# A graph layer pair on one core: first rows in smaller pieces, factors moved to GpSimd, conversions of the adjacency tiles one pair closer to their use

## The chip, the cores and the metric

The kernel runs on 1 core of a Trainium2 chip. The metric is the device time of one execution in microseconds (us). The profile shown is that of one execution of the kernel before.

## The reference

Inputs are x (4096 x 128, float32), adj (4096 x 4096, zeros and ones with the diagonal set), a scalar beta, and two 128 x 128 weights.

```python
h = relu(layernorm(x))
norm2 = norm(h, axis=1, keepdims=True)
cos = beta[0] * (h @ h.T) / (norm2 @ norm2.T + 1e-07)
P = softmax(cos + (1.0 - adj) * -1e9, axis=1)
x = x + P @ h
h = relu(layernorm(x))
deg = clip(sum(adj, axis=1, keepdims=True), 1.0)
x = x + h @ W_self + (adj @ h / deg) @ W_neigh
```

## The kernel before

Two stages follow each other. The first is an attention over the adjacency's edges, the second an aggregation `adj @ h` with two small products. TensorE works nearly all the time in both.

**The front.** x comes in four pieces of 8 tiles (a tile is 128 rows). VectorE computes mean and variance of each piece (`variances`, L640), GpSimd raises variance + eps to the power -1/2 (`inverse_std`, L376), VectorE multiplies by a constant factor and makes the bias (`scales`, L652), ScalarE makes the rows of h (L512), VectorE sums their squares (`norms`, L660), GpSimd raises these to -1/2 (`inverse_norm`, L382). A "unit" is a group of 4 tiles of h divided by their norms; there are 8, made by GpSimd (0, 7), ScalarE (3) and VectorE (the others). TensorE transposes each, ScalarE and VectorE split it into a high and a low 16-bit part (`unit_high` L503, `unit_low` L678). When all norms are known, their smallest one decides by a flag (`s_flag`, L437 to L442) which of two forms of the attention ScalarE and VectorE run. The general form is not run with these inputs. ScalarE's and VectorE's first attention instructions stand behind that flag. GpSimd also makes the low half of a table of h (`low_parts`, L369) after ScalarE has made the high half (`table_high`, L522).

**The attention** goes over 72 pairs k. The adjacency is symmetric in its use of the scores: a pair (s, p) joins 512 rows of step s with 256 rows of pair p. A pair whose rows lie in a later step is used in both directions ("far"), and has two 512 KB tiles of the adjacency, a near and a far one; a pair within its own step has only the near one. Step s starts at pair 0, 16, 30, 42, 52, 60, 66, 70. In step 0 the own pairs come first. In the later steps own pairs stand at the third and the fifth place of the step, pairs 18 and 20 in step 1.

For each k in turn:
- SP loads the near tile, and the far tile right behind it (L323 to L334). Near tiles have two slots, so the load of near tile k waits until near tile k-2 has been converted (L327).
- GpSimd converts near tile k+3 to fp8 behind its masking of pair k (`convert(k + LEAD)`, L479, with `LEAD = 3`), and every second far tile (`convert_far`). ScalarE converts the other far tiles (`convert`, L530): that of pair k+2 behind the exponentials of pair k (L588).
- TensorE computes the scores of pair k+2 (L941), multiplies the far words (L979 to L982), transposes words of pair k+1 (L952), multiplies the near words (L1002 to L1005).
- ScalarE computes the exponentials twice, in 16 and 32 bits (L561, L562). Those of pair k wait until GpSimd has masked pair k-2 (L552).
- VectorE subtracts them into a low part (`low_part`, L778), masks far words (`mask_far`, L788), adds finished far rows (L803). Its order for one k is low part of the first chunk of k+2, spill of k, `mask_far` of k+1, low part of the second chunk of k+2.
- GpSimd masks the near words (`mask_near`, L407). Behind it stand the table parts, the conversions, and at the fifth pair of a step (k = 20 in step 1) the five small instructions of `scales_of_x2` (L456).
- Score banks: the first score chunk of a pair waits for the low part of the last chunk two pairs before, the second for that of the first chunk of the pair before (`ring_free`, L909, where no unit stands between).

ScalarE's second layernorm (`second_h`) has its first half behind the exponentials of the seventh pair of a step (k = 22 in step 1), and its second half with `second_high` behind those of the eighth, k = 23, after the conversion that stands there.

Of the kernel before, what the change touches and what calls it, by code (L numbers as in the profile page):

```python
# [5 lines left out]
def gnn_program(nc, x_in, adj_in, beta_in, w_self_in, w_neigh_in, out):  # L6
# [7 lines left out]
    T = N // P  # L14
# [9 lines left out]
    RING = [("unit", 0), ("unit", 1), ("score", 0, 0), ("score", 0, 1), ("score", 1, 0), ("score", 1, 1), ("unit", 2)]  # L24
# [18 lines left out]
    XP = 4  # L43
    TX = T // XP
    LEAD = 3
# [6 lines left out]
    with ctx:  # L52
# [36 lines left out]
        var_e, rstd, scale_h, bias_h, norm2, norm2_g, rnorm, rnorm_s = [early(7, T) for _ in range(8)]  # L89
# [6 lines left out]
        def u_rows(a, b):  # L96
            half, lo = u_half[a * 2 // T], a * 2 // T * (T // 2)
            return half[:, (a - lo) * D:(b - lo) * D]

# [89 lines left out]
        def transpose_bank(g):  # L189

            return 5 + AT["unit", g] % 3
# [72 lines left out]
        s_rnorm_s = sem("rnorm_scaled")  # L264
# [47 lines left out]
        def _(sp):  # L312
            sp.dma_start(beta, beta_in.partition_broadcast(P)).then_inc(s_beta, 16)
            for i in range(XP):
                sp.dma_start(x_v3[:, TX * i:TX * (i + 1), 0:D], x_v[:, TX * i:TX * (i + 1), :]).then_inc(s_x[i], 16)

# [6 lines left out]
            tile = 0  # L323
            for k in range(NP):
                s = PAIR[k][0]
                if k >= 2:
                    sp.wait_ge(s_adjd, k - 1)  # L327
                sp.dma_start(stage[:, k % 2 * TILE:(k % 2 + 1) * TILE], adj_in[tile]).then_inc(s_near_in[k % 2], 16)
                tile += 1
                if PAIR[k][2]:  # L330
                    m = FAR_BEFORE[k]
                    if m >= 2:
                        sp.wait_ge(far_sem(m), m // 2)
                    sp.dma_start(stage[:, (2 + m % 2) * TILE:(3 + m % 2) * TILE], adj_in[tile]).then_inc(s_far_in[m % 2], 16)  # L334
                    tile += 1
# [20 lines left out]
        def _(pool):  # L356
# [19 lines left out]
            def inverse_std(i):  # L376

                part = slice(i * TX, (i + 1) * TX)
                pool.wait_ge(s_var, i + 1)
                pool.tensor_tensor(rstd[:, part], var_e[:, part], neg_half, ALU.pow).then_inc(s_rstd, 1)  # L380

            def inverse_norm(i):  # L382

                part = slice(i * TX, (i + 1) * TX)
                pool.wait_ge(s_norm2, i + 1)
                pool.tensor_tensor(rnorm[:, part], norm2_g[:, part], neg_half, ALU.pow).then_inc(s_rnorm, 1)

            def scaled_inverse_norm(i):

                pool.wait_ge(s_rnorm, i + 1)  # L390
                pool.tensor_scalar(rnorm_s[:, i * TX:(i + 1) * TX], rnorm[:, i * TX:(i + 1) * TX], HS, None, ALU.mult
                                   ).then_inc(s_rnorm_s, 1)
# [16 lines left out]
            def units(g):  # L409

                pool.wait_ge(s_rnorm, g * TPS // TX + 1)
                for t in range(g * TPS, (g + 1) * TPS):
                    pool.tensor_scalar(u_rows(t, t + 1), h_rows(t, t + 1), rnorm[:, t:t + 1], HS, ALU.mult, ALU.mult
                                       ).then_inc(s_unit_p, 1)

            def convert_far(k):
# [3 lines left out]
                if m == FAR_BEFORE[FIRST[2]]:  # L420
# [79 lines left out]
        def _(act):  # L500
# [7 lines left out]
            for i in range(XP):  # L508
                act.wait_ge(s_scales, i + 1)
                for t in range(i * TX, (i + 1) * TX):  # L510
# [3 lines left out]
                if i == XP - 2:  # L514
# [707 lines left out]
```

## Time and profile before

| | us |
|---|---|
| median of 3 runs | 504.44 |
| lowest, highest | 503.09, 505.62 |
| the profiled execution | 502.87 |
| its span, from first to last instruction | 500.9 |
| TensorE busy in the span | 471.2 |
| VectorE, ScalarE, GpSimd busy | 279.8, 298.1, 297.0 |

The 2.0 us between the span and the profiled execution's time lie around the first and the last instruction. An engine's busy time is an average over a front in which TensorE waits, an attention and an aggregation in which it does not; what matters for a change is where in the trace TensorE is idle.

### The profile page before, as it was taken

How to read it: one execution, taken by the hardware profiler on the slowest of the kernel's cores; microseconds unless marked ns; L12 is line 12 of the kernel's file. 1: busy time of each engine (PE TensorE's matmuls, PEld its weight loads, DVE VectorE, ACT ScalarE, POOL GpSimd, SP SyncE). 2: the span in 40 equal slices, each digit the busy share in tenths (PEclk: the TensorE clock that was granted, in tenths of full speed). 3: DMA queues.
4: the chain of work that ended last, by engine and by line, in shares of the span. 5: the costliest groups of instructions: out<-in, count | busy, mean ns of one | idle time of the engine just before them, and what ended most of it. 6: DMA issues, size and time to landing. Idle time of an engine off the chain costs nothing.

```text
span 500.9 us, 12746 instructions
## 1 busy us (share of the span) xinstructions
PE 471.2 (94%) x5392; PEld 397.7 (79%) x5392; DVE 279.8 (56%) x686; ACT 298.1 (60%) x427; POOL 297.0 (59%) x261
## 2 busy tenths in 40 slices
PE   0768999999999999999999999999799999999996
PEld 0636788888788888888888888877688888888895
DVE  6975666567566585656765856757632321322153
ACT  2979787866986759876798598688730201110121
POOL 3889887877897768986799688888750000000000
PEclk9989999999999999999999999999999999999999
DMA  8057865655776557754676476563010000000001
GB/s 248 12 183 282 273 204 175 224 178 183 252 249 221 181 161 249 245 217 157 225 244 236 167 227 223 205 196 107 3 34 1 22 22 22 1 22 22 22 1 43
DMA packets 31549, 74.39 MB, mean 149 GB/s; under 512 B 2560, under 2 KB 15104, under 8 KB 31488
## 3 DMA queue, kind: packets, MB, share of 16 engines
q1 hardware_dynamic: 31488, 73.54, 43.8%
q8 instruction: 42, 0.69, 0.6%
q14 instruction: 19, 0.16, 0.1%
HBM read 71.43 MB, written 2.10 MB: 147 GB/s over the span
## 4 chain that ended last, share of the span: by engine, by line
PE 87%; DVE 5%; POOL 3%; DMA 2%; ACT 2%; issue 1%; SPq 0%; POOLq 0%; DVEq 0%; ACTq 0%
PE ps L1078 23%; PE ps L941 17%; PE ps L952 9%; PE ps L1005 6%; PE ps L1002 6%; PE ps L1004 6%; PE ps L979 5%; PE ps L982 5%; PE ps L981 5%; PE ps L1063 2%; PE ps L1052 2%; DVE adj_t L665 1%; DVE adj_t L644 1%; DMA stage<-in_adj_dram 1%; DMA x_sb<-in_x_dram 1%
## 5 line engine op out<-in xcount | busy, mean ns | idle before, releaser
L407 POOL TENSOR_TENSOR near<-word,adj_t 128x1024 f32<-128x1024 f32 x72 | 145.2, 2016 | 57.4 <-DVE word L778 56.4
L561 ACT ACTIVATE word<-ps,small 128x512 f16<-128x512 f32 x144 | 135.6, 942 | 70.8 <-PE ps L941 67.0
L778 DVE TENSOR_TENSOR word<-ps,word 128x512 f16<-128x512 f32 x144 | 106.3, 739 | 105.4 <-ACT ps L562 105.3
L1078 PE MATMUL ps<-table,adj_t 128*128 128x257 f16 x1024 | 116.8, 274 | 0.0
L941 PE MATMUL ps<-unit_t 128*128 128x512 f16 x432 | 106.7, 381 | 4.7 <-DVE word L778 4.7
L1078 PEld LDWEIGHTS ps<-table,adj_t 128*128 128x128 fp8e4 x1024 | 99.3, 98 | 13.0
L562 ACT ACTIVATE ps<-ps,small 128x512 f32<-128x512 f32 x144 | 107.2, 744 | 0.0
L1002 PE MATMUL ps<-table,near 128*128 128x129 f16 x576 | 102.6, 219 | 4.0 <-POOL near L407 2.6
L1005 PE MATMUL ps<-table,near 128*128 128x129 f16 x576 | 102.8, 222 | 0.0
L1004 PE MATMUL ps<-table,near 128*128 128x128 f16 x576 | 102.6, 219 | 0.0
L979 PE MATMUL ps<-table,far 128*128 128x129 f16 x448 | 79.9, 219 | 0.3
L982 PE MATMUL ps<-table,far 128*128 128x129 f16 x448 | 80.0, 222 | 0.0
L981 PE MATMUL ps<-table,far 128*128 128x128 f16 x448 | 79.8, 219 | 0.0
L788 DVE TENSOR_TENSOR far<-ps,adj_t 128x1024 f32<-128x1024 f32 x56 | 68.4, 1222 | 14.0 <-PE ps L952 14.0
L398 POOL TENSOR_SCALAR adj_t<-stage 128x1024 uint8<-128x1024 f32 x72 | 75.4, 1047 | 0.6
L616 ACT ACTIVATE stage<-ps 128x1024 f16<-128x1024 f16 x15 | 14.6, 1021 | 101.8 <-PE ps L1052 101.8
L941 PEld LDWEIGHTS ps<-unit_t 128*128 128x128 f16 x432 | 39.4, 98 | 41.6 <-DVE word L778 7.9
L1002 PEld LDWEIGHTS ps<-table,near 128*128 128x128 f16 x576 | 57.0, 99 | 6.4 <-POOL near L407 2.7
L952 PE MATMUL ps<-ident,word 128*128 128x128 f32 x448 | 58.3, 273 | 0.0
L1004 PEld LDWEIGHTS ps<-table,near 128*128 128x128 f16 x576 | 55.9, 97 | 2.0
L1005 PEld LDWEIGHTS ps<-table,near 128*128 128x128 f16 x576 | 56.3, 98 | 0.0
L979 PEld LDWEIGHTS ps<-table,far 128*128 128x128 f16 x448 | 44.4, 99 | 10.4 <-DVE far L788 5.7
(94 smaller groups left out, 490.6 us busy)
## 6 DMA issues: line engine op xcount, KB each, us to landing
stage<-in_adj_dram SPq DMA_DIRECT2D x128, 512.0 KB, 4.4
x_sb<-in_x_dram SPq DMA_DIRECT2D x4, 512.0 KB, 6.2
x_again<-in_x_dram SPq DMA_DIRECT2D x8, 256.0 KB, 5.6
out_dram<-x_sb SPq DMA_DIRECT2D x7, 256.0 KB, 2.3
out_dram<-x_sb SPq DMA_DIRECT2D x1, 192.0 KB, 2.0
stage<-in_L_gnn_W_neigh_dram SPq DMA_DIRECT2D x1, 64.0 KB, 2.6
stage<-in_L_gnn_W_self_dram SPq DMA_DIRECT2D x1, 64.0 KB, 2.5
out_dram<-x_sb SPq DMA_DIRECT2D x1, 64.0 KB, 1.7
```

The source lines that it names most:

```text
L407: pool.tensor_tensor(ring(near, k), ring(word, k), adj_t[:, near_adj(k)], ALU.mult).then_inc(s_near, 1)
L561: act.activation(half(word16, k, c, 0, HIGH, TPS), score(k, c), ACT.Exp, bias=exp_bias, scale=exp_scale)
L562: act.activation(score(k, c), score(k, c), ACT.Exp, bias=exp_bias, scale=exp_scale).then_inc(s_exp, 1)
L778: dve.tensor_tensor(half(word16, k, c, 0, LOW, TPS), score(k, c), half(word16, k, c, 0, HIGH, TPS), ALU.subtract).then_inc(s_elo, 1)
L941: ins = pe.matmul(score(k, c), j, rows, start=i == 0, stop=i == 2)
L979: pe.matmul(far_acc(c), high, tab(rows, D, TW), start=c == 0 and t == 0, stop=False, skip_group_check=True)
L981: pe.matmul(far_acc(c, 0, D), high, tab(rows, 0, D), start=False, stop=False, skip_group_check=True)
L982: last = pe.matmul(far_acc(c), low, tab(rows, D, TW), start=False, stop=t == TPS - 1, skip_group_check=True)
L1002: pe.matmul(acc(s, t), high, tab(rows, D, TW), start=first and c == 0 and t % 2 == 0, stop=False, skip_group_check=True)
L1004: pe.matmul(acc(s, t, 0, D), high, tab(rows, 0, D), start=False, stop=False, skip_group_check=True)
L1005: last = pe.matmul(acc(s, t), low, tab(rows, D, TW), start=False, stop=end and c == 1, skip_group_check=True)
L1078: return pe.matmul(ps[:, agg_bank(g) + t, 0:TW], adj_t[:, at:at + P], tab(b), start=(b == 0), stop=(b == T - 1))
```

## The change

x is loaded in five pieces, two of 4 tiles and three of 8. The constant factors of the inverse deviation and the inverse norm move into an instruction of GpSimd ahead of each power, so that VectorE's and GpSimd's separate scaling instructions go. Units 0, 5 and 6 are made by ScalarE (5 and 6 inside the attention), 1 to 4 by VectorE (3 and 4 behind the flag), 7 by GpSimd at k = 6. The first table part is made ahead of the flag, and the later ones one pair earlier or later than before on GpSimd. The first two far tiles are loaded with the first two near ones. The first three transposes use other banks. `LEAD` goes from 3 to 2.

```diff
-    RING = [("unit", 0), ("unit", 1), ("score", 0, 0), ("score", 0, 1), ("score", 1, 0), ("score", 1, 1), ("unit", 2)]
+    RING = [("score", 0, 0), ("score", 0, 1), ("score", 1, 0), ("score", 1, 1)]
...
-    XP = 4
-    TX = T // XP
-    LEAD = 3
+    PIECE = [slice(0, 4), slice(4, 8), *(slice(t, t + 8) for t in range(8, T, 8))]
+    XP = len(PIECE)
+    GROUPS = [p.stop // TPS for p in PIECE]
+    LEAD = 2
...
+            load_near(0)
+            load_near(1)
+            load_far(FAR[0])
+            load_far(FAR[1])
+            for k in range(2, NP):
+                sp.wait_ge(s_adjd, k - 1)
+                load_near(k)
+                m = FAR_BEFORE[k]
+                if PAIR[k][2] and m >= 2:
+                    sp.wait_ge(far_sem(m), m // 2)
+                    load_far(k)
...
             def inverse_std(i):
-                pool.tensor_tensor(rstd[:, part], var_e[:, part], neg_half, ALU.pow).then_inc(s_rstd, 1)
+                pool.tensor_scalar(var_e[:, part], mv_v[:, part, 1], HS ** -2, EPS * HS ** -2, ALU.mult, ALU.add
+                                   ).then_inc(s_scaled_e, 1)
+                pool.wait_ge(s_scaled_e, i + 1)
+                pool.tensor_tensor(scale_h[:, part], var_e[:, part], neg_half[:, 0:part.stop - part.start], ALU.pow
+                                   ).then_inc(s_rstd, 1)
...
             inverse_std(2)
             inverse_norm(0)
-            units(0)
+            inverse_norm(1)
             inverse_std(3)
-            inverse_norm(1)
-            scaled_inverse_norm(1)
             convert(0)
+            inverse_std(4)
             inverse_norm(2)
+            convert(1)
...
+            low_parts(0)
             inverse_norm(3)
-            units(7)
-            convert(1)
-            convert(2)
-            convert_far(2)
+            inverse_norm(4)
...
                 mask_near(k)
-                if s == 0 and k % 2 == 0:
-                    low_parts(k // 2)
+                if k == 1:
+                    convert_far(2)
+                if s == 0 and k % 2 == 1 and (k + 1) // 2 < NS:
+                    low_parts((k + 1) // 2)
+                if k == 6:
+                    units(7)
                 if k + LEAD < NP:
                     convert(k + LEAD)
-                    if PAIR[k + LEAD][2] and FAR_BEFORE[k + LEAD] % 2 == 0:
+                    if k >= 1 and PAIR[k + LEAD][2] and FAR_BEFORE[k + LEAD] % 2 == 0:
                         convert_far(k + LEAD)
...
+            first_h(0, 0, 4)
+            first_h(1, 4, 8)
+            first_h(2, 8, 12)
+            units(0)
+            first_h(2, 12, 16)
+            unit_high(0)
+            first_h(3, 16, 24)
+            first_h(4, 24, T)
+            act.wait_ge(s_h, TPS)
+            table_high(0)
             act.wait_ge(s_flag, 1)
...
-                    if k == 1:
-                        unit_high(2)
+                    if k <= 1:
+                        unit_high(k + 1)
...
+                    if k in (3, 5):
+                        units((k + 7) // 2)
...
             norms(0)
             scales(2)
+            norms(1)
             variances(3)
-            norms(1)
             scales(3)
+            variances(4)
             norms(2)
-            units(1)
             unit_low(0)
+            scales(4)
             norms(3)
+            norms(4)
...
-            unit_low(1)
-            units(2)
+            units(1)
             dve.wait_ge(s_flag, 1)
             any_small = dve.value_load(small_norm[0:1, :], min_val=0, max_val=1)
-            units(4)
-            units(5)
-            units(6)
+            units(2)
...
                     low_part(k, 0)
+                    units(3 + k)
                     low_part(k, 1)
-                unit_low(2)
+                    unit_low(1 + k)
...
-            sum_of_h(0, TX)
+            sum_of_h(0, 8)
             unit_transpose(0)
-            sum_of_h(TX, T - TX)
+            sum_of_h(8, 16)
+            scores(0)
+            for i in range(3):
+                score_product(1, 0, i)
+            sum_of_h(16, T)
             unit_transpose(1)
-            scores(0)
-            sum_of_h(T - TX, T)
-            scores(1)
-            unit_transpose(2)
+            for i in range(3):
+                score_product(1, 1, i)
...
                     scores(k + 2)
+                    if k == 0:
+                        unit_transpose(2)
```

## Rows read from the trace of the kernel before

**Rows 1.** The page: TensorE's busy time and share.
```profile
PE 471.2 (94%) x5392; PEld 397.7 (79%) x5392; DVE 279.8 (56%) x686; ACT 298.1 (60%) x427; POOL 297.0 (59%) x261
```

**Rows 2.** Windows: stretch, its length, busy us per engine, clock, DMA share, GB/s.
```profile
50.00:60.00 10.00, 10.00 (x125) 8.40 (x123) 6.14 (x10) 7.96 (x11) 9.03 (x7) 1.00 0.81 285
```

**Rows 3.** Timeline of the front: start us, us, engine, line, operation, count.
```profile
5.59 1.64 DVE L644 BATCH_NORM_STATS2 adj_t<-x_sb 128x6 f32<-128x128 f32 x8 [0.59 <-DMA x_sb<-in_x_dram]
7.27 0.64 DVE L647 BATCH_NORM_AGGREGATE adj_t<-adj_t 128x2 f32<-128x6 f32 x8
...
10.88 9.35 ACT L512 ACTIVATE adj_t<-x_sb,adj_t 128x128 f32<-128x128 f32 x24 [8.86 <-DVE adj_t L657]
...
20.99 3.19 ACT L512 ACTIVATE adj_t<-x_sb,adj_t 128x128 f32<-128x128 f32 x8 [0.28 <-DVE adj_t L657]
...
27.08 0.15 DVE L710 TENSOR_SCALAR small<-small 128x1 f32<-128x1 f32 x1
...
28.80 0.92 ACT L561 ACTIVATE word<-ps,small 128x512 f16<-128x512 f32 x1 [1.52 <-POOL small L441]
```

**Rows 4.** GpSimd by line and form: count, busy us, mean ns, idle before.
```profile
L407 POOL TENSOR_TENSOR near<-word,adj_t 128x1024 f32<-128x1024 f32 x72 | 145.2, 2016 | 57.4 <-DVE word L778 56.4 <-PE ps L1005 0.9
L398 POOL TENSOR_SCALAR adj_t<-stage 128x1024 uint8<-128x1024 f32 x72 | 75.4, 1047 | 0.6
L424 POOL TENSOR_SCALAR adj_t<-stage 128x1024 uint8<-128x1024 f32 x28 | 29.3, 1046 | 0.0
L373 POOL TENSOR_TENSOR table<-adj_t,table 128x512 f16<-128x512 f32 x8 | 9.1, 1133 | 0.0
...
L465 POOL TENSOR_TENSOR small<-small 128x4 f32<-128x4 f32 x8 | 8.1, 1014 | 0.7
L386 POOL TENSOR_TENSOR adj_t<-adj_t,small 128x8 f32<-128x8 f32 x4 | 6.6, 1660 | 0.7 <-DVE adj_t L669 0.6
...
L391 POOL TENSOR_SCALAR adj_t<-adj_t 128x8 f32<-128x8 f32 x1 | 0.3, 288 | 0.1
```

**Rows 5.** Timeline: one VectorE instruction beside a conversion on GpSimd.
```profile
22.62 1.05 POOL L398 TENSOR_SCALAR adj_t<-stage 128x1024 uint8<-128x1024 f32 x1
...
22.69 1.01 DVE L669 TENSOR_SCALAR adj_t<-adj_t 128x8 f32<-128x8 f32 x1
```

**Rows 6.** The far tiles' loads, L334: time from issue to landing.
```profile
DMA to landing us min/median/max: 3.7/4.7/6.9
```

**Rows 7.** Timeline of step 1 on GpSimd, ScalarE and VectorE, pairs 21 to 24.
```profile
133.17 1.05 POOL L398 TENSOR_SCALAR adj_t<-stage 128x1024 uint8<-128x1024 f32 x1
...
136.40 2.01 POOL L407 TENSOR_TENSOR near<-word,adj_t 128x1024 f32<-128x1024 f32 x1
...
138.44 0.93 ACT L561 ACTIVATE word<-ps,small 128x512 f16<-128x512 f32 x1 [0.47 <-POOL near L407]
...
141.33 1.06 ACT L538 ACTIVATE adj_t<-stage 128x1024 uint8<-128x1024 f32 x1
...
143.72 0.91 ACT L561 ACTIVATE word<-ps,small 128x512 f16<-128x512 f32 x1
...
145.26 0.74 DVE L778 TENSOR_TENSOR word<-ps,word 128x512 f16<-128x512 f32 x1 [2.43 <-ACT ps L562]
...
146.23 1.20 DVE L788 TENSOR_TENSOR far<-ps,adj_t 128x1024 f32<-128x1024 f32 x1
```

**Rows 8.** The chain that ended last, in steps 0 and 1: start, us, what.
```profile
50.33 1.41 PE ps L941 x6
...
147.06 1.29 PE ps L941 x6
```

**Rows 9.** Timeline at the like places of steps 2 and 6.
```profile
206.25 1.06 ACT L538 ACTIVATE adj_t<-stage 128x1024 uint8<-128x1024 f32 x1
...
333.65 1.05 POOL L398 TENSOR_SCALAR adj_t<-stage 128x1024 uint8<-128x1024 f32 x1
...
337.56 1.10 ACT L538 ACTIVATE adj_t<-stage 128x1024 uint8<-128x1024 f32 x1
```

More of the change, by code:

```diff
@@ L88, in gnn_program @@
         mv = early(7, T * 2)
-        var_e, rstd, scale_h, bias_h, norm2, norm2_g, rnorm, rnorm_s = [early(7, T) for _ in range(8)]
+        var_e, scale_h, bias_h, norm2, norm2_g, rnorm = [early(7, T) for _ in range(6)]
         ones_w = early(6, P)
@@ L98, in u_rows, with piece_of @@
             return half[:, (a - lo) * D:(b - lo) * D]
+        mv_v = mv.rearrange("p (t c) -> p t c", c=2)
+        def piece_of(g):
+            return min(i for i in range(XP) if GROUPS[i] > g)
         def by_tile(ap):
@@ L189, in transpose_bank @@
         def transpose_bank(g):
[L191 removed]
+            return (3, 4, 2)[g] if g < 3 else 5 + AT["unit", g] % 3
         def tab(t, lo=0, hi=TW):
@@ L321, in load_x_again, with load_near, load_far @@
                 sp.dma_start(by_tile(x_again[:, :]), x_v[:, s * TPS:(s + 1) * TPS, :]).then_inc(s_xr, 16)
[L323 to L335, printed above, removed]
+            def load_near(k):
+                sp.dma_start(stage[:, k % 2 * TILE:(k % 2 + 1) * TILE], adj_in[k + FAR_BEFORE[k]]).then_inc(s_near_in[k % 2], 16)
+            def load_far(k):
+                m = FAR_BEFORE[k]
+                sp.dma_start(stage[:, (2 + m % 2) * TILE:(3 + m % 2) * TILE], adj_in[k + m + 1]).then_inc(s_far_in[m % 2], 16)
+            load_near(0)
[5 more added lines that the diff above has]
+                load_near(k)
+                m = FAR_BEFORE[k]
+                if PAIR[k][2] and m >= 2:
+                    sp.wait_ge(far_sem(m), m // 2)
+                    load_far(k)
                 for again in range(NS):
@@ L642, in variances @@
                 dve.wait_ge(s_x[i], 16)
-                for t in range(i * TX, (i + 1) * TX):
+                for t in range(PIECE[i].start, PIECE[i].stop):
                     last = dve.bn_stats(stats[:, t * 6:(t + 1) * 6], x_row(t))
                 then(last)
-                for t in range(i * TX, (i + 1) * TX):
+                for t in range(PIECE[i].start, PIECE[i].stop):
                     last = dve.bn_aggr(mv[:, t * 2:(t + 1) * 2], stats[:, t * 6:(t + 1) * 6])
-                then(last)
-                dve.tensor_scalar(var_e[:, i * TX:(i + 1) * TX], mv_v[:, i * TX:(i + 1) * TX, 1], EPS, None,
-                                  ALU.add).then_inc(s_var, 1)
+                last.then_inc(s_var, 1)
             def scales(i):
-                part = slice(i * TX, (i + 1) * TX)
+                part = PIECE[i]
+                dve.wait_ge(s_var, i + 1)
                 dve.wait_ge(s_rstd, i + 1)
-                then(dve.tensor_scalar(scale_h[:, part], rstd[:, part], HS, None, ALU.mult))
                 dve.scalar_tensor_tensor(bias_h[:, part], mv_v[:, part, 0], -1.0, scale_h[:, part],
@@ L660, in norms @@
             def norms(i):
-                part = slice(i * TX, (i + 1) * TX)
-                for t in range(i * TX, (i + 1) * TX):
+                for t in range(PIECE[i].start, PIECE[i].stop):
                     dve.wait_ge(s_h, t + 1)
@@ L667, in norms @@
                         scale=1.0, scalar=0.0, op0=ALU.mult, op1=ALU.add, accum_out=norm2[:, t:t + 1])
-                then(last)
-                dve.tensor_scalar(norm2_g[:, part], norm2[:, part], 1e-20, None, ALU.max).then_inc(s_norm2, 1)
+                last.then_inc(s_norm2, 1)
             def units(g):
-                dve.wait_ge(s_rnorm, g * TPS // TX + 1)
+                dve.wait_ge(s_rnorm, piece_of(g) + 1)
                 for t in range(g * TPS, (g + 1) * TPS):
-                    dve.tensor_scalar(u_rows(t, t + 1), h_rows(t, t + 1), rnorm[:, t:t + 1], HS,
-                                      ALU.mult, ALU.mult).then_inc(s_unit, 1)
+                    dve.tensor_scalar(u_rows(t, t + 1), h_rows(t, t + 1), rnorm[:, t:t + 1], None, ALU.mult).then_inc(s_unit, 1)
             def unit_low(g):
```

59 lines of the change are left out of this document (30 added, 29 removed).

## The prediction

> **What bounds the kernel now.** I read the busy times, then the windows, then the timeline of the front, then one later step engine by engine. TensorE is busy 471.2 of 500.9 us [rows 1], and from about 50 us on a window of the attention is full, 10.00 of 10.00, with ScalarE at 7.96 and GpSimd at 9.03 [rows 2]. The change leaves TensorE's work as it is. So there are only two ways to the time: the point at which TensorE's unbroken work begins moves, or a stall opens in it. As marker of the first I take the end of the scores of pair 5, 50.33 + 1.41 = 51.74 [rows 8].
>
> The reader is to see in the later step [rows 7] how close the helpers run. GpSimd masks pair 21 from 136.40 to 138.41, ScalarE had waited 0.47 us for it and begins its exponentials of pair 23 at 138.44, converts the far tile of pair 25 at 141.33 without a wait, and starts pair 24 at 143.72. A far tile takes 4.7 us (3.7 to 6.9) from issue to landing [rows 6]. Conversions are made three pairs ahead, so this tile was asked for well before.
>
> **Part 1: the front.** The time of a piece follows its parts. VectorE's statistics of 8 tiles take 7.27 + 0.64 - 5.59 = 2.3 us [rows 3], of 4 tiles 1.25. A power is 1.66 us for 8 columns and 1.01 for 4; with the factor instruction now ahead of it (0.29) and the hops between, 2.15 and 1.4 [rows 4]. The first piece is half as large, so VectorE can start between 5.0 and 5.59; I take 5.0.
> - Statistics of piece 0 to 6.3, power to 7.7, first row of h at 8.0, against 10.88 [rows 3].
> - Piece 1: power to 9.0. Piece 2: statistics to 10.2, power to 12.35. GpSimd then makes the powers of norms 0 and 1, to 15.0. These are one more than before at this place.
> - Piece 3: VectorE does its statistics behind the norms of piece 1, to 15.7; power to 17.9. VectorE now stands in `scales(3)` and waits for it, since the statistics of piece 4 come behind. They end at 20.4, their power at 22.55, and ScalarE makes the last eight rows from 22.9, 3.19 long [rows 3], to 26.1. Before they ended at 20.99 + 3.19 = 24.18.
> - The last squares, the minimum and its sign take 0.8 more: 26.9, against 27.08 + 0.15 = 27.23 [rows 3]. So the early start of 2.9 us is used up before the flag. I call this point L.
>
> One thing can make L later. An 8-column instruction of VectorE took 1.01 us and ended with a 1.05 us conversion of GpSimd beside it [rows 5]; the one of L710 took 0.15 [rows 3]. The moved `convert(1)` now runs beside VectorE's norms, so L lies between 26.9 and 26.9 + 1.0. I take 27.2.
>
> The Trainium skill (SBUF — State Buffer, Who interferes with whom) speaks against this placing: the second port pair is an exclusive lock that GpSimd shares with two-input instructions of VectorE, and the later one blocks fully. The row agrees in size. By the rule L would be 27.9 and the total 0.7 higher; without it 0.3 lower.
>
> From L on GpSimd is the longer way. It has, one behind the other [rows 3, 4]: the flag 0.7 (estimated from 27.23 to ScalarE's start at 28.80, of which the flag is the first half), a table part 1.13, two powers of 2.07, masking of pair 0 2.02, a conversion 1.05, masking of pair 1 2.02, a far conversion 1.05, a table part 1.13, conversion of tile 3 1.05. Sum 14.2, thus 41.4. Only then are near and far tile 5 asked for. Issue 0.4 and landing 4.7 [rows 6] give 46.5, ScalarE's conversion 1.0 gives 47.5. From the start of the exponentials to the second low part VectorE needs (145.26 - 143.72) + (146.23 - 145.26) + 1.20 + 0.65 = 4.4 [rows 7], and the second half of the scores 0.65. The marker falls at 52.5, against 51.74: **0.8 later**, with L's bounds 0.5 to 1.5, and down to -0.5 if the tile lands in 3.7.
>
> Units 5 and 6 on ScalarE are four activations of 0.4 each (3.19 / 8) [rows 3], 1.6 a time. The first four stand ahead of the wait for tile 5, which hides them; uncovered they cost 1.6. The second four, at pair 5, delay ScalarE by less than it idles per pair (10.00 - 7.96 in ten us, [rows 2]) and VectorE's `mask_far` of the pair before is later than they are: 0, uncovered 1.6. Unit 7 on GpSimd is under 2 us at pair 6, where masking has several us before TensorE needs it: 0, uncovered 2. VectorE loses two to three small instructions a piece, which is in the sum above; units 3 and 4 behind the flag run while it waits for exponentials. The two early far tiles remove nothing at the marker, since tile 5 is later.
>
> **Part 2: LEAD 3 to 2.** SP asks for near tile k, and the far one behind it, when tile k-2 is converted. That conversion stood behind the masking of pair k-5 and now stands behind that of pair k-4. ScalarE's conversion of far tile k stands behind its exponentials of k-2, which themselves need only the masking of k-4. So exponentials (141.33 - 138.44 = 2.89 us) run against conversion, issue and landing (1.05 + 0.4 + 4.7 = 6.15). Where ScalarE starts right when the mask ends, it waits 3.2 us. In the regular part it starts some 3.5 us behind the mask, which leaves a wait of a few tenths in its idle time: 0. Behind the two own pairs of a step, where TensorE needs little time, it starts at once (the 0.47 of rows 7).
>
> Step 1 in full [rows 7]. At pair 20 GpSimd converts till 134.22, then makes the five small instructions of the second layernorm, and masks pair 21 at 136.40. With the new lead a far conversion (1.05) belongs here too: pair 22's instead of none. Mask 21 runs 137.45 to 139.46, conversion of 23 to 140.5, far tile 25 is issued at 140.9 and lands at 145.6. ScalarE converts it to 146.55; the second layernorm's rows behind it take 143.72 - 141.33 - 0.96 = 1.43; pair 24 starts at 148.0 instead of 143.72, 4.3 later. VectorE's low part moves from 145.26 to 149.55, its far masking to 150.5, with end at 151.7. TensorE was ready for that product at 147.06 + 1.29 = 148.35 [rows 8]. Loss: **3.35 us**. Bounds: without the extra far conversion 2.3, with landing in 3.7 another 1.0 less, thus 1.3; with 6.9 it is 5.5.
>
> The same place is there in steps 2, 3 and 4 (first 206.25, [rows 9]), the pattern of pairs being the same: 4 x 3.35 = 13.4. In step 6 the tile of pair 68 is behind a conversion that ends at 333.65 + 1.05 = 334.7, and lands at 339.8, 2.2 us after ScalarE asks for it at 337.56 [rows 9]. The helpers bound there already: **2.2** (0 to 3.3).
>
> **Sum.** 502.87 + 0.8 + 13.4 + 2.2 = 519.3 for the profiled execution. The median of the runs is 1.57 above that execution, so I move halfway, to **520**.
>
> **The rivals.**
> - The tiles come sooner. Landing in 3.7 and no push of mask 21 by the far conversion give 1.3 a step, 1.2 in step 6 and 0.3 in front: 502.87 + 5.2 + 1.5 = 509.6, with the half step to the median 510. For: 3.7 occurs; against: that the far load goes out right behind the near one here. Chance 0.18.
> - The waits are there and hidden. TensorE has scores two pairs ahead, so ScalarE might catch up: only the front's 0.8 is left, 504 to 505. For: no wait of TensorE in these windows before; against: VectorE's 1.20 us far masking ends at 147.4, only 0.9 ahead of TensorE's need. Chance 0.12.
> - Faster: the early rows carry through. h starts 2.9 us sooner; if the fifth piece follows without VectorE's wait in `scales(3)` and tile 5 is there in time, the whole front moves, 504.4 - 2.9 = 501.5. It decides at the flag: it must come at 25 us or earlier, and the steps must not stall. For: 10.88 becomes 8.0; against: the last row's 26.1. Chance 0.08.
> - The tiles come later still, near 6.9, as near and far share the DMA engines: 5.5 a step, 527. Chance 0.07.
> - My forecast: 0.55, own range 515 to 523.
>
> Faster and slower are counted from 0.5%, 2.5 us, about what a measurement of this kernel can tell from no change. Faster 0.08; same 0.12; slower 0.55 + 0.18 + 0.07 = 0.80. The range is 506 to 523: it leaves out the hidden and the faster case at the low end. They hold 0.20.
>
> **What would show it.** Each step: first h row at 8.0; last at 26.1; ScalarE's L538 waits for the DMA 3 us or more at the conversions of pairs 25, 39, 51 and 61, and about 2 at 68; TensorE then waits for VectorE's `far` (L788) some 3 us, four times; the other windows stay full. Wrong it is if ScalarE's conversions show no wait for the DMA, or if they wait and TensorE's gaps don't grow, or if the flag comes before 25 us.

## The result, and the profile after

The changed kernel takes 534.07 us (532.20 to 535.95, 6 runs) against 504.31 (502.81 to 505.62, 6 runs): a ratio of 1.0595, interval 1.0574 to 1.0617. The forecast was 520 with a range of 506 to 523. The sign was right, the size was not: 30 us were lost, not 16. The profiled execution took 532.20 us, its span 530.4 against 500.9. Of all 79 recorded executions of the kernel before, all but four lie in one of two groups, 502.6 to 503.4 us and 504.1 to 504.8, and its profiled one is of the lower.

The page after, its busy times and the head of its chain of waits, to be read beside [rows 1]:

```profile
PE 483.0 (91%) x5392; PEld 403.1 (76%) x5392; DVE 279.4 (53%) x671; ACT 299.8 (57%) x435; POOL 298.5 (56%) x268
...
PE 63%; POOL 9%; DVE 9%; DMA 8%; ACT 5%; issue 4%; SPq 0%; ACTq 0%; POOLq 0%; DVEq 0%
```

TensorE has the same 5392 products and is counted busy for 483.0 us instead of 471.2. So of the 29.5 us of span, 17.7 are idle time, and in 11.8 the same products take longer. The ends of products are modelled in a profile, so the 11.8 are no clean measure of any one cause; what the lower clock costs is worked out below from starts. The transfers of the adjacency now make 8% of the chain.

Where the time went is read best from one event that both kernels have 72 times, the start of ScalarE's exponentials (L561 before, L591 after). This is the delay against before in us, worked out from the timelines; the last row is the end of the span. The other columns are experiments of the next section.

```
                        forecast  after   e1     e2     e3     e4
after the front (k=6..20)   0.8    5.98   3.48   2.65   3.02   3.87
gained in step 1 (k=27)     3.35   5.60   0.00   5.64   0.40   4.72
gained in step 2 (k=43)     3.35   3.25   0.00   3.27   1.80   3.34
gained in step 3 (k=53)     3.35   3.86   0.00   3.57   0.35   3.78
gained in step 4 (k=62)     3.35   5.71   0.00   5.48   0.48   3.36
gained in step 6 (k=69)     2.2    3.36   0.28   2.24   0.66   3.24
the rest, to the end        0      1.7   -0.2    0.4    0.2    0.4
```

**The stalls are where they were forecast.** ScalarE's conversions of far tiles by line, and the five that were named (start, length, and in brackets the wait and what ended it):

```profile
L568 ACT ACTIVATE adj_t<-stage 128x1024 uint8<-128x1024 f32 x28 | 29.7, 1061 | 31.1 <-DMA stage<-in_adj_dram 31.0
```

```profile
152.31 1.06 ACT L568 ACTIVATE adj_t<-stage 128x1024 uint8<-128x1024 f32 x1 [3.89 <-DMA stage<-in_adj_dram]
...
221.78 1.06 ACT L568 ACTIVATE adj_t<-stage 128x1024 uint8<-128x1024 f32 x1 [2.83 <-DMA stage<-in_adj_dram]
...
280.68 1.06 ACT L568 ACTIVATE adj_t<-stage 128x1024 uint8<-128x1024 f32 x1 [2.90 <-DMA stage<-in_adj_dram]
...
330.68 1.06 ACT L568 ACTIVATE adj_t<-stage 128x1024 uint8<-128x1024 f32 x1 [4.22 <-DMA stage<-in_adj_dram]
...
365.36 1.06 ACT L568 ACTIVATE adj_t<-stage 128x1024 uint8<-128x1024 f32 x1 [3.02 <-DMA stage<-in_adj_dram]
```

They are the tiles of pairs 25, 39, 51, 61 and 68, 16.9 of the 31.0 us of waiting. The other eleven waits, 14.1 us together, are not in the forecast's sum. They seem to have fallen mostly into time in which ScalarE is otherwise idle, for steps 2 and 3 lost about what was forecast. The chain of waits of the changed kernel in step 1 (start, us, what) goes just the way of the forecast, from GpSimd's masking over its conversion and the load to ScalarE and to VectorE's far masking:

```profile
143.43 2.00 POOL near L424
...
145.50 1.06 POOL adj_t L415
146.58 0.33 SPq L333
146.95 5.33 DMA stage<-in_adj_dram
152.31 1.06 ACT adj_t L568
153.37 0.78 ACT unit_t L599 x2
...
157.26 1.14 DVE far L814
```

The far load went out at 146.95: the forecast had 140.9, and with the front's 5.98 that is 146.9. It took 5.33 us against an assumed 4.7.

**What the forecast has no term for** is in the windows of the same place (stretch, its length, busy us of PE, PEld, DVE, ACT, POOL, then the clock that TensorE was granted, the DMA share and GB/s):

```profile
150.00:152.00 2.00, 2.00 (x32) 1.99 (x30) 0.00 (x0) 0.00 (x0) 2.00 (x2) 1.00 0.93 315
152.00:154.00 2.00, 1.83 (x24) 1.22 (x21) 0.00 (x0) 1.69 (x3) 1.55 (x2) 1.00 0.98 375
154.00:156.00 2.00, 0.00 (x0) 0.00 (x0) 0.00 (x0) 1.97 (x4) 0.00 (x0) 1.00 0.82 207
156.00:158.00 2.00, 0.82 (x3) 0.21 (x3) 1.77 (x3) 2.00 (x4) 0.00 (x0) 0.97 0.87 344
158.00:160.00 2.00, 1.55 (x15) 1.55 (x16) 1.78 (x3) 2.00 (x4) 0.88 (x1) 0.50 0.06 23
```

TensorE does nothing from 154 to 156 and little to 158. Work resumes, and now the granted clock is 0.50, the lower of its two levels (1.2 instead of 2.4 GHz). What that does to the work is seen best on equal work. TensorE's timeline shows 24 far products and then the transposes, first here and then in e4, an experiment of the next section in which the clock stays at 1.00 in this place:

```profile
158.45 0.29 PE L1009 MATMUL ps<-table,far 128*128 128x129 f16 x1 [0.61 <-DVE far L814]
...
161.01 1.19 PE L982 MATMUL ps<-ident,word 128*128 128x128 f32 x8
```

```profile
156.78 0.23 PE L1016 MATMUL ps<-table,far 128*128 128x129 f16 x1 [0.61 <-DVE far L814]
...
158.17 1.04 PE L989 MATMUL ps<-ident,word 128*128 128x128 f32 x8
```

From the first far product to the transposes it is 2.56 us here and 1.39 there. In step 4 and behind the last pair the clock falls too. The last two rows show the latter place: TensorE is idle from 388 to 390, and then the clock is 0.50:

```profile
334.00:336.00 2.00, 0.61 (x2) 0.28 (x3) 1.39 (x3) 2.00 (x4) 0.00 (x0) 0.85 0.75 305
336.00:338.00 2.00, 2.00 (x14) 1.18 (x13) 1.94 (x3) 2.00 (x4) 0.51 (x1) 0.50 0.00 0
...
388.00:390.00 2.00, 0.00 (x0) 0.00 (x0) 1.86 (x8) 1.88 (x5) 2.00 (x2) 1.00 0.00 0
390.00:392.00 2.00, 1.94 (x19) 1.94 (x20) 1.06 (x8) 0.41 (x1) 1.36 (x4) 0.50 0.35 107
```

**The front**, against [rows 3], in the timeline of the changed kernel (the rows follow each other by engine: ScalarE, VectorE, GpSimd):

```profile
8.35 1.65 ACT L532 ACTIVATE adj_t<-x_sb,adj_t 128x128 f32<-128x128 f32 x4 [6.32 <-DVE adj_t L686]
...
23.91 3.19 ACT L532 ACTIVATE adj_t<-x_sb,adj_t 128x128 f32<-128x128 f32 x8 [1.46 <-DVE adj_t L686]
```

```profile
18.19 1.04 DVE L686 SCALAR_TENSOR_TENSOR adj_t<-adj_t 128x8 f32<-128x8 f32 x1 [2.11 <-POOL adj_t L398]
...
28.41 0.15 DVE L739 TENSOR_SCALAR small<-small 128x1 f32<-128x1 f32 x1
...
35.82 2.76 DVE L702 TENSOR_SCALAR adj_t<-adj_t 128x128 f32<-128x128 f32 x4
```

```profile
18.17 1.05 POOL L415 TENSOR_SCALAR adj_t<-stage 128x1024 uint8<-128x1024 f32 x1
...
35.12 2.00 POOL L424 TENSOR_TENSOR near<-word,adj_t 128x1024 f32<-128x1024 f32 x1
...
37.20 1.11 POOL L415 TENSOR_SCALAR adj_t<-stage 128x1024 uint8<-128x1024 f32 x1
```

The first row of h comes at 8.35 (forecast 8.0), the last at 27.1 (26.1), the point L at 28.56 (27.2, before 27.23). And the four instructions of unit 4, which take 0.86 us elsewhere, take 2.76 beside a mask and a conversion of GpSimd. Unit 3 took 0.86.

### The profile page after: what moved, and what is told of

The parts are those of the page before. It is cut to its first block, busy times and chain, and to the rows that moved or that the text cites. A ratio compares the mean times of both kernels' runs of the same rounds, so it can differ in the third digit from the quotient of the medians.

```text
span 530.4 us, 12752 instructions
## 1 busy us (share of the span) xinstructions
PE 483.0 (91%) x5392; PEld 403.1 (76%) x5392; DVE 279.4 (53%) x671; ACT 299.8 (57%) x435; POOL 298.5 (56%) x268
## 4 chain that ended last, share of the span: by engine, by line
PE 63%; POOL 9%; DVE 9%; DMA 8%; ACT 5%; issue 4%; SPq 0%; ACTq 0%; POOLq 0%; DVEq 0%
PE ps L1112 21%; PE ps L971 9%; DMA stage<-in_adj_dram 7%; PE ps L982 6%; POOL near L424 5%; PE ps L1035 4%; PE ps L1009 4%; PE ps L1032 4%; PE ps L1012 4%; PE ps L1034 4%; PE ps L1011 3%; ACT word L591 3%; DVE far L814 2%; PE ps L1097 2%; POOL adj_t L415 2%
## 5 line engine op out<-in xcount | busy, mean ns | idle before, releaser
L591 ACT ACTIVATE word<-ps,small 128x512 f16<-128x512 f32 x144 | 134.6, 935 | 65.5 <-PE ps L971 60.9
L971 PE MATMUL ps<-unit_t 128*128 128x512 f16 x432 | 111.3, 390 | 22.5 <-DVE word L804 17.7
L1032 PE MATMUL ps<-table,near 128*128 128x129 f16 x576 | 103.8, 221 | 4.1 <-POOL near L424 2.8
L1035 PE MATMUL ps<-table,near 128*128 128x129 f16 x576 | 104.0, 224 | 0.0
L1034 PE MATMUL ps<-table,near 128*128 128x128 f16 x576 | 103.8, 221 | 0.0
L1009 PE MATMUL ps<-table,far 128*128 128x129 f16 x448 | 83.0, 224 | 3.7 <-DVE far L814 3.3
L1012 PE MATMUL ps<-table,far 128*128 128x129 f16 x448 | 82.9, 227 | 0.0
L1011 PE MATMUL ps<-table,far 128*128 128x128 f16 x448 | 82.8, 224 | 0.0
```

What stands on the lines that cost most here:

```text
L591: act.activation(half(word16, k, c, 0, HIGH, TPS), score(k, c), ACT.Exp, bias=exp_bias, scale=exp_scale)
L971: ins = pe.matmul(score(k, c), j, rows, start=i == 0, stop=i == 2)
L1009: pe.matmul(far_acc(c), high, tab(rows, D, TW), start=c == 0 and t == 0, stop=False, skip_group_check=True)
L1011: pe.matmul(far_acc(c, 0, D), high, tab(rows, 0, D), start=False, stop=False, skip_group_check=True)
L1012: last = pe.matmul(far_acc(c), low, tab(rows, D, TW), start=False, stop=t == TPS - 1, skip_group_check=True)
L1032: pe.matmul(acc(s, t), high, tab(rows, D, TW), start=first and c == 0 and t % 2 == 0, stop=False, skip_group_check=True)
```

## The experiments

My theory after the result had two parts. (a) `LEAD = 2` is nearly all of it: the far tile's load goes out too late, since it stands on SP behind a near load that waits for a conversion; a stall costs more than its idle time, because TensorE's clock falls behind it. (b) The front loses the rest, by the later L and by units on VectorE beside GpSimd's masks. The main rival of (a) was contention: two more tiles in flight, or the other edits of the attention, and not the lead.

**e1: the whole change but with three pairs of lead**, with the third conversion ahead of the loop as before.

```diff
-    LEAD = 2
+    LEAD = 3
...
             inverse_norm(4)
+            convert(2)
```

> The changed kernel with LEAD back at 3 (the conversion of tile 2 stands ahead of the loop again), all else as changed. Theory (the far tile that ScalarE waits for is asked for one pair too late): ScalarE's waits for the DMA at pairs 25, 39, 51, 61 and 68 go, and with them the 11.58 - 5.98 = 5.6, 3.25, 3.9, 5.7 and 3.35 us that these steps lose in the changed kernel, and most of the 1.8 at the end; what stays is the front's loss of up to 6 us. That gives 508 to 511 us. Rival (the steps' loss comes from the moved units, table parts or factors): the time stays above 525.

Measured: 508.36 (506.48 to 510.11), ratio 1.0092, interval 1.0060 to 1.0125. The steps lose nothing but 0.28 in step 6 (column e1); what is left is the front's 3.5. The lead is 534.07 - 508.36 = 25.7 us of the 29.8.

**e2: the reverse, only the lead changed in the kernel before.**

```diff
-    LEAD = 3
+    LEAD = 2
...
             convert(1)
-            convert(2)
-            convert_far(2)
```

> The kernel before with LEAD = 2 alone (conversion of tiles 2 and far 2 inside the loop). Theory: the steps lose what they lose in the changed kernel, 20 to 24 us, and the front little: 524 to 530 us. Rival (the loss needs the new order of the other work): under 510.

Measured: 530.39 (526.08 to 533.46), ratio 1.0542, interval 1.0491 to 1.0593. The median lies 0.4 above my bound. ScalarE's conversions in it, by line:

```profile
L536 ACT ACTIVATE adj_t<-stage 128x1024 uint8<-128x1024 f32 x28 | 29.7, 1062 | 35.9 <-DMA stage<-in_adj_dram 35.9
```

35.9 us of waiting, where the changed kernel has 31.0. The contention rival falls: none of the other edits is in this kernel, and its steps lose nearly the same amounts. The granted clock fell in steps 1 and 4 here too, and those two cost 5.6 and 5.5 against 3.3 and 3.6 for steps 2 and 3.

**e3: two pairs of lead, but SP asks for the far tile ahead of the near one.** The conversions stay as late as in the changed kernel, only the far load no longer stands behind the near load's wait.

```diff
-                sp.wait_ge(s_adjd, k - 1)
-                load_near(k)
                 m = FAR_BEFORE[k]
                 if PAIR[k][2] and m >= 2:
                     sp.wait_ge(far_sem(m), m // 2)
                     load_far(k)
+                sp.wait_ge(s_adjd, k - 1)
+                load_near(k)
```

> The changed kernel with LEAD = 2, but SP issues the far tile's load ahead of the near tile's wait, so that it hangs on its own slot alone and no longer on GpSimd's conversion of near tile k-2. Theory: it is the position of the load in SP's queue, not GpSimd's later conversion by itself, that makes ScalarE wait. The waits of ScalarE for the DMA at L568 go to about 0, and the time to 508 to 513 (front 4 to 6, and about 1 a step for the mask that a far conversion pushes). Rival (GpSimd's later conversions and masks hold ScalarE and TensorE): above 525.

Measured: 512.04 (509.64 to 513.61), ratio 1.0168, interval 1.0134 to 1.0202. 22 of the 25.7 us come back by a change of order in one queue. The far load of pair 25 goes out at 139.60 in SP's timeline, and the near one, now behind it, waits for its own slot till 143.58 without holding this far load up; below it ScalarE's conversions by line, with 5.0 us of waiting instead of 31.0:

```profile
139.60 0.50 SPq L338 DMA_DIRECT2D stage<-in_adj_dram  x1
143.58 0.33 SPq L333 DMA_DIRECT2D stage<-in_adj_dram  x1
```

```profile
L568 ACT ACTIVATE adj_t<-stage 128x1024 uint8<-128x1024 f32 x28 | 29.9, 1066 | 5.1 <-DMA stage<-in_adj_dram 5.0
```

What is left against e1, some 3.7 us, is the price of conversions one pair nearer to their use. The rest was the far load's place in the queue.

**e4: does the clock's fall have a price of its own?** In steps 1 and 4 the same stall is left, but TensorE repeats score products (12 more, ahead of the scores of pairs 25 and 61, into a bank that these overwrite), so that it is idle for less of it.

```diff
+                    if k in (23, 59):
+                        ring_free("score", k + 2, 0)
+                        for _ in range(4):
+                            for i in range(3):
+                                score_again(k + 2, 0, i)
                     scores(k + 2)
```

> The changed kernel in which TensorE repeats the first chunk's score products four times (12 matmuls, 2.6 us at full clock) ahead of the scores of pairs 25 and 61, the places of steps 1 and 4 where it otherwise stands idle 3 us and its granted clock falls to 0.50. The repeats write the same values and are not in the reference's work. Theory (steps 1 and 4 lose 5.6 and 5.7 us against 3.25 and 3.9 in steps 2 and 3 because of the clock): the clock stays at 1.0, each of the two steps loses 3.3 to 3.8, and the kernel is about 4 us faster than the changed one, 530 us. Rival (those two steps lose more because their tile lands later): no gain, 534 to 535.

Measured: 527.56 (525.38 to 529.50), ratio 1.0479, interval 1.0442 to 1.0515: 6.5 us faster than the changed kernel with 24 products more. The windows of this kernel in step 1:

```profile
154.00:156.00 2.00, 1.00 (x5) 0.21 (x3) 1.45 (x3) 2.00 (x4) 0.00 (x0) 1.00 0.90 332
156.00:158.00 2.00, 1.39 (x23) 1.23 (x23) 1.93 (x3) 2.00 (x3) 0.56 (x1) 1.00 0.14 55
```

The granted clock stays 1.00. The price of the clock can be read from how a step's delay goes on behind its stall: first the delay of the first exponentials behind it (pair 24, 38 or 60), then that of the pairs after (27, 43, 62), each gained within its step, in us, from the timelines.

```
clock fell to 0.50:   after, step 1  5.00 -> 5.60    after, step 4  5.48 -> 5.71
                      e2, step 1     4.98 -> 5.64    e2, step 4     4.75 -> 5.48
clock stayed at 1.00: after, step 2  3.96 -> 3.25    e2, step 2     3.96 -> 3.27
                      e4, step 1     5.43 -> 4.72    e4, step 4     4.03 -> 3.36
```

Where the clock stays, 0.7 us of the delay is made up again. (Step 3 isn't in the list: the clock stays there too, and 0.45 is made up in each of the three runs, from a first delay that reads 0.2 too small, since pair 50 starts that much sooner than in the kernel before in the kernels without a stall as well.) Where it falls, 0.2 to 0.7 is added. So a fall costs 0.9 to 1.4 us beside the idle time, in the changed kernel 1.3 in step 1 and 0.9 in step 4: 2.2, where I had expected 4. The starts of equal work say the same of step 1: from the first far product to the next near one 3.59 us at the lower clock, 2.27 in e4. The rest of the 6.5 us isn't the filler's: in this execution the tile of pair 61 came 1.4 us sooner and that of pair 25 0.4 later, and the clock stayed up in the front and behind the last pair too, where this kernel's code is the changed kernel's (1.6 and 1.4 us; 0.5 more in the front is an earlier tile, with which TensorE's idle time there is shorter by as much). So the same code may or may not be followed by the low clock. That the filler is what kept it up in steps 1 and 4 is likely, since it fell in both steps in the changed kernel and in e2, but one profile of each kernel doesn't show it.

**e5 to e7: the front, with three pairs of lead.** e5 moves VectorE's units 3 and 4 behind both low parts, to let GpSimd's masks start sooner:

```diff
                     low_part(k, 0)
-                    units(3 + k)
                     low_part(k, 1)
                     unit_low(1 + k)
+                    units(3 + k)
```

e6 is e5 with `convert_far(2)` at k = 0 instead of 1. e7 is e6 with `variances(4)` ahead of `scales(3)`, so that VectorE doesn't stand in the wait of 2.11 us shown above.

> The changed kernel with LEAD = 3, and VectorE's units 3 and 4 moved behind both low parts and the unit's low half. In the run with LEAD = 3 alone units 4 took 3.50 us for four instructions beside GpSimd's masking of pair 0 and a conversion (0.86 to 0.88 where nothing of that kind ran), which held the low part, mask 1, far conversion 2 and with them the load of tile 5. Theory: those 2.6 us are on the front's path; mask 1 comes 2 us sooner, ScalarE's wait of 2.30 us for tile 5 mostly goes, the front's loss falls from 3.5 to about 1.5 us: 506.0 to 506.8. Rival (tile 5 is late because of SP's order behind far tile 4, whatever the units do): no gain, 508.

> As the run before, with the conversion of far tile 2 behind mask 0 instead of mask 1, in GpSimd's idle time. SP's load of far tile 4 waits for it, and near and far tile 5 stand behind that load. Theory: far tile 5 is asked for another 2 us sooner and ScalarE waits for nothing: 505 to 506. Rival (the front's loss is the later flag, 28.4 against 27.2, alone): no difference to the run before.

> As the run before, with VectorE's statistics of the last piece ahead of scales(3) instead of behind it, so that it does not wait 2.1 us for the power of piece 3 with the statistics undone. Theory: the last row of h is there about 2 us sooner (25.0 instead of 27.1), the flag too, and the front gains 1.5 to 2: 503 to 504.5, as fast as the kernel before or slightly faster. Rival (GpSimd's chain of powers behind the flag sets the front, and these powers wait for norms that come no sooner): no gain.

Measured: e5 508.80 (507.47 to 509.23), e6 509.25 (507.50 to 509.46), e7 506.43 (505.26 to 507.43). e5 and e6 brought nothing against e1's 508.36: my theory that the units only had to stand behind the low parts fell. The timeline of VectorE in e7, then GpSimd's, shows what stands there in its place:

```profile
37.52 4.75 DVE L703 TENSOR_SCALAR adj_t<-adj_t 128x128 f32<-128x128 f32 x4
```

```profile
37.10 1.04 POOL L415 TENSOR_SCALAR adj_t<-stage 128x1024 uint8<-128x1024 f32 x1
38.10 1.99 POOL L424 TENSOR_TENSOR near<-word,adj_t 128x1024 f32<-128x1024 f32 x1
40.06 1.12 POOL L388 TENSOR_TENSOR table<-adj_t,table 128x512 f16<-128x512 f32 x1
41.15 1.04 POOL L415 TENSOR_SCALAR adj_t<-stage 128x1024 uint8<-128x1024 f32 x1
```

Four instructions of 0.21 us take 4.75 us, and they end as GpSimd's fourth one does, which looks like one of theirs for each of its. Moved behind the low parts they only met more of GpSimd's work. e7 gained 2.8 us on e6, of which the earlier L is 2.2 (26.45 instead of 28.61), and missed the 503 to 504.5 that I gave it. That the units are why is the theory that e9 tests.

**e8: the early first far tiles alone, in the kernel before.**

```diff
+            load_near(0)
+            load_near(1)
+            load_far(FAR[0])
+            load_far(FAR[1])
+            for k in range(2, NP):
```

> The kernel before with one part of the change alone: the first two far tiles are loaded with the first two near ones, ahead of any wait. In the kernel before ScalarE waited 1.46 us for far tile 3 in the front, on the chain that ended last. Theory: that wait goes and TensorE's unbroken work begins 1 to 1.4 us sooner: 502.9 to 503.4. Rival (the next tiles' loads or conversion 2 then bind at once): within 0.3 us of 504.3.

Measured: 503.25 (501.86 to 504.72), ratio 0.9986, interval 0.9972 to 1.0000. From pair 5 on the exponentials start 0.7 us sooner than before. A wait of 1.46 us for the second far tile is gone. In the median that is at the edge of what can be told from nothing. In e8's profile the clock falls behind the last pair and 1.6 us is lost there, as in the changed kernel's profile, though none of its steps stalls. The profiles of e10, e11 and e12 have that fall too; those of the kernel before, e1 to e7 and e9 don't.

**e9 and e10: the units away from the masks.** Unit 3 directly behind unit 2, unit 4 by ScalarE at k = 1; e9 starts from e7 with e5's move taken back, e10 from e1. ("The run before the last", in what was expected of e9, is e7.)

```diff
             units(2)
+            units(3)
...
-                    units(3 + k)
...
-                    if k in (3, 5):
+                    if k in (1, 3, 5):
                         units((k + 7) // 2)
```

> The changed kernel with three pairs of lead, the fifth piece's variances before scales(3) and the far conversion at pair 0 (as the run before the last), but units 3 and 4 no longer on VectorE beside GpSimd's masks: unit 3 is made right behind unit 2, unit 4 by ScalarE at pair 1. Theory (units on VectorE beside long GpSimd instructions cost about one such instruction each, 4.7 us for four on the way to the second low part): most of those 4.7 us goes, exponentials of pair 7 on start within 1 us of the kernel before, 502.5 to 504.0. Rival (the units only filled time in which VectorE waited for something else, and four activations of 0.4 us on ScalarE now delay it by as much): 505.5 to 507.0, as in the run that it starts from (506.4).

> The changed kernel with three pairs of lead (508.4) and only the same move of units 3 and 4. It parts the front's loss of 3.5 to 3.7 us in two: by the theory the units' share is about 2.5 us and the later flag's about 1.2, so 505.3 to 506.3 here. Rival (the later flag and the powers behind it are the whole loss): 507.5 to 509.

Measured: e9 504.20 (503.57 to 506.05), ratio 1.0012, interval 0.9995 to 1.0029; e10 506.03 (505.23 to 508.28), ratio 1.0050, interval 1.0032 to 1.0068. Against e7 and e1 that is 2.2 and 2.3 us. e9's rival falls, and its interval stays clear of e7's (1.0033 to 1.0069). e10's median lies where the theory has it, but its interval overlaps e1's, and its profile doesn't confirm the gain: the exponentials there lag by 4.35 us behind the front, more than e1's 3.48, with the clock at 0.50 from 46 to 48, where e1's stayed at 1.00. So e9 carries this result. e9 lies 0.2 above my bound: ScalarE is now busy in all of the 2 us windows from 38 to 50, with the four activations (1.26 us) among its work.

**e11: unit 4 on VectorE again, but beside GpSimd's power.** As e9, without ScalarE's unit at k = 1, and with these lines:

```diff
                     low_part(k, 0)
+                    if k == 0:
+                        units(4)
                     low_part(k, 1)
```

> As the run before (units 3 and 4 not beside masks, 504.2), but unit 4 is made by VectorE again, between the two low parts of pair 0, where GpSimd raises 128x8 to a power instead of masking. Theory (it is the long two-input and one-input instructions of GpSimd that hold VectorE up, its powers don't): the four take 0.9 to 1.1 us here, the low part behind them is hidden by GpSimd's powers, and ScalarE is rid of four activations (1.26 us) ahead of the exponentials of pair 2: 502.8 to 503.8. Rival (any GpSimd instruction holds the units up): the four take 1.9 us or more, and the run is at 504 or above.

VectorE's row of the unit, and GpSimd's two beside it:

```profile
30.47 0.86 DVE L703 TENSOR_SCALAR adj_t<-adj_t 128x128 f32<-128x128 f32 x4
```

```profile
30.42 0.36 POOL L405 TENSOR_SCALAR adj_t<-adj_t 128x8 f32<-128x8 f32 x1
30.86 1.79 POOL L408 TENSOR_TENSOR adj_t<-adj_t,small 128x8 f32<-128x8 f32 x1
```

0.86 us for the four: a power of GpSimd doesn't hold them up, the masks and conversions did. In its profile the exponentials of pair 2 start 1.16 us sooner than in e9 and those of pair 7 1.1 sooner, as expected. The median, 504.45 (503.35 to 505.00), ratio 1.0005, interval 0.9991 to 1.0019, doesn't confirm a gain over e9 (1.0012): the intervals overlap. The effect on the unit is shown, its worth is not.

**e12: e11 with ScalarE's order at k = 1 changed**: the table part and the conversion run where it waited 1.84 us for the transposes of unit 2.

```diff
-                    if k <= 1:
-                        unit_high(k + 1)
+                    if k == 0:
+                        unit_high(1)
...
                         convert(k + 2)
+                    if k == 1:
+                        unit_high(2)
```

> As e11, and ScalarE's high part of unit 2 behind its table part and conversion of pair 1 instead of ahead of them, since it waited 1.74 us there for TensorE's transposes. If ScalarE is what sets the front after the units are gone (100% busy from 38 to 51 us), the exponentials of pair 2 start 1 to 1.6 us sooner: 501.5 to 502.6, faster than both kernels. Rival: the later unit 2 holds up the scores of pair 4 and gives it back, 503 or above.

```profile
34.77 1.09 ACT L569 ACTIVATE adj_t<-stage 128x1024 uint8<-128x1024 f32 x1
36.38 0.60 ACT L526 ACTIVATE unit_t<-ps 128x512 f16<-128x512 f32 x1 [0.53 <-PE ps L964]
36.87 0.92 ACT L592 ACTIVATE word<-ps,small 128x512 f16<-128x512 f32 x1
```

ScalarE's timeline shows the wait down to 0.53 and the exponentials of pair 2 at 36.87, against 38.62 in the kernel before. From pair 6 on it leads the kernel before by 1.07 us. The median is 503.44 (501.95 to 504.85), ratio 0.9984, interval 0.9969 to 1.0000. That is 30.6 us better than the changed kernel. Against the kernel before it is about the same lead as e8's, at the edge of what can be told.

## Why the prediction was right in sign and wrong in size

I go through the prediction's steps in the profiled execution, whose span grew by 29.5 us; 16.4 were forecast and 13.1 are missing. The missing part falls into four pieces: 3.8 us of lower clock in the front and two steps, 4.0 in the steps' tiles, 3.6 in the front beside the clock, and 1.7 behind the last pair, nearly all of it a fall of the clock that the change need not have caused.

- **The late far load: right.** Place, cause and order of events were as forecast, in all five places, and the term of 3.35 measured 3.25 and 3.86 in steps 2 and 3. e1 and e2 show that the lead is the cause, e3 that it works through the far load's place behind the near load's wait. The hidden rival fell: ScalarE did not catch up.
- **The sentence that failed: "The change leaves TensorE's work as it is. So there are only two ways to the time"**, a later start or a stall. There was a third, the same products at half the clock behind a stall, and the sum has no term for it. It is 1.3 in step 1, 0.9 in step 4 and 1.6 in the front: 3.8 of the missing 13.1. Another 1.4 is the fall behind the last pair. That one needs no stall: e8, e10, e11 and e12 have it in their profiles with no step stalled. e8 is the kernel before but for its first loads, so that the profiled execution of the kernel before had none is likely chance. [Rows 2] show a window at 1.00: there was no long stall behind which the clock could fall, and the sum took every duration from there.
- **Tiles that came later than 4.7 us: 4.0 more over the steps.** The far tile of pair 25 took 5.33 and the first exponentials behind it came 5.0 late, not 4.3; that of pair 61 was waited for 4.22 us, that of pair 68 3.02 instead of 2.2 (step 6: 3.4 instead of 2.2). Without the clock each term lies within its bounds in the forecast (up to 5.5), save step 6's 3.36, just above 3.3. The 4.7 was the median of all landings in [rows 6]. From the start of their issue the five tiles took 5.3, 4.3, 4.4, 5.9 and 5.8 us, so it was fair for pairs 39 and 51 and short for the three others. The issuing instructions of those three lasted 0.97, 1.35 and 1.31 us in SP's timeline, against 0.43 and 0.44. Why is open; in e4 the tile of pair 61 landed in 4.5.
- **Part 1, the front: 0.8 forecast, 6.0 measured**, 4.4 without the clock, the term that was furthest off. GpSimd's chain of work, given till 41.4, ended at 44.45. Of this, 1.4 are L (28.56 instead of 27.2), and 1.0 is a wait of GpSimd for the low part that stood behind unit 4. I had given one conversion of GpSimd beside VectorE's squares a price (up to 1.0, of which I took 0.3). Two conversions struck: `scales(3)` took 1.04 instead of 0.19, and one square 1.16 instead of 0.28.
- **"Units 3 and 4 behind the flag run while it waits", priced at nothing: wrong.** Unit 4 took 2.76 beside the masks. Taking both units away from there gave back 2.2 us in e9, which had the conversions three pairs ahead. [Rows 5] had shown the effect on one small instruction. I applied it to the squares and not to the units, which are four instructions, each of which can be caught.
- **The range.** Its top of 523 is not worked out in the prediction, and its own rival of late tiles, 527 at a chance of 0.07, lay above it. 534 is nearest to that rival. A clock term for five stalls, about 1 us each, would have taken the rival to 532.
- From the profiled execution to the median the runs lie 1.9 us higher (534.07 against 532.20). The profiled execution was the fastest of the six and had the highest mean granted clock, 0.983 against 0.971 to 0.978. So in the others the lower clock probably cost more than the trace shows; no trace of them was kept.

## What to carry to other kernels

A load whose buffer is free must not stand in a queue behind one that waits: order the two by when their buffers come free, before you shorten a lead. Where a change opens a stall in TensorE's work, add to the idle time a price for running at 1.2 GHz behind it, here 0.9 to 1.4 us for each fall in a step. And ask of each VectorE instruction between buffers of SBUF that moves which GpSimd instruction will run beside it: the four instructions of one unit took 0.86 us beside a power and 4.75 beside a mask, a table part and two conversions.

And before two profiles are subtracted, look for events that one execution happened to have and the other not, as the fall of the clock behind the last pair: 1.4 of the 29.5 us here.

## What the runs showed of the hardware

- The clock after a stall isn't a matter of the idle time alone. In the changed kernel TensorE is idle for 2.93 us in the windows from 282 to 288 (step 3), and the clock stays 1.00. In the front it is idle for 2.45 us from 52 to 56 and the clock falls to 0.50. Behind the last pair it idles 2.47 us from 386 to 390, and the clock falls; in the kernel before the same place has 2.57 idle from 358 to 362 and keeps 1.00, in its windows:

```profile
360.00:362.00 2.00, 0.04 (x1) 0.04 (x2) 1.90 (x8) 1.97 (x5) 1.91 (x1) 1.00 0.00 0
362.00:364.00 2.00, 2.00 (x30) 1.94 (x31) 1.74 (x11) 0.27 (x1) 1.49 (x3) 1.00 0.26 66
```

  e8 has the same 2.57 us of idle time in the same windows, and there the clock falls:

```profile
362.00:364.00 2.00, 2.00 (x19) 1.74 (x17) 1.25 (x8) 0.00 (x0) 1.83 (x3) 0.51 0.58 171
```

  What decides is open.
- VectorE's 128x128 multiplication by a column (fp32, SBUF to SBUF) took 4.75 us for four beside a conversion, a mask, a table part and a conversion of GpSimd (e7), about one of these instructions each, and 0.86 for four beside its 128x8 power (e11). The Trainium skill (SBUF — State Buffer, Who interferes with whom) says that the shared port pair is held for a whole instruction and the other engine fully blocks. The first number agrees with it. The second does not fit the rule as it is worded, for the power reads SBUF too; it took 1.79 us there, against 1.67 for the one before it.
- VectorE's subtractions from PSUM kept their 0.71 to 0.74 us beside masks of the same kind, so only part of its work is exposed.
